# An LSTM layer on one core: twelve plain steps for sixteen, and one sigmoid for three gates of half the features

## The reference

```python
# x (32, 512, 512), h0 = cond_1024 (32, 512), Wx and Wh (512, 2048), b (2048,)
xW = jnp.einsum('ntd,dk->tnk', x, Wx) + b
def step(carry, xw_t):
    prev_h, prev_c = carry
    a = xw_t + prev_h @ Wh
    i = sigmoid(a[:, :H]); f = sigmoid(a[:, H:2*H]); o = sigmoid(a[:, 2*H:3*H])
    g = tanh(a[:, 3*H:])
    next_c = f * prev_c + i * g
    next_h = o * tanh(next_c)
    return ((next_h, next_c), next_h)
_, hs = lax.scan(step, (h0, 0), xW)
out = x + transpose(hs, (1, 0, 2))
```

## Time and profile before

| | |
|---|---|
| median of 3 runs | 2535.98 us (2535.93 to 2538.73) |
| the profiled execution's own time | 2535.94 us |
| its span | 2534.1 us |
| TensorE busy | 2515.8 us, 99% of the span |
| VectorE busy | 1983.6 us, 78% |
| ScalarE busy | 1247.9 us, 49% |
| chain that ended last | TensorE 98%, VectorE 1% |

### The profile page before, as it was taken

The page is one execution under the profiler, slowest core; times in us unless marked ns, Lnnn a source line. Parts: engine busy times, 40 slices in busy tenths (PEclk is TensorE's granted clock), DMA queues, the critical chain, the costliest instruction groups (busy, mean ns, idle before and its releaser), DMA issues.

```text
span 2534.1 us, 155783 instructions
## 1 busy us (share of the span) xinstructions
PE 2515.8 (99%) x67134; PEld 1795.3 (71%) x67134; DVE 1983.6 (78%) x8602; ACT 1247.9 (49%) x5266; POOL 7.2 (0%) x12
## 2 busy tenths in 40 slices
PE   8999999999999999999999999999999999999998
PEld 3577777777777777777777777777777777777775
DVE  7877777777777777777777777777777777777776
ACT  6544444444444444444444444444444444444443
POOL 1000000000000000000000000000000000000000
PEclk9999999999999999999999999999999999999999
DMA  8101101101011011010110110101101001011000
GB/s 234 37 20 30 33 17 33 28 21 33 17 33 33 17 33 25 24 33 17 33 33 17 33 25 25 33 17 33 33 17 33 25 25 33 17 33 33 17 17 18
DMA packets 142169, 80.21 MB, mean 32 GB/s; under 512 B 8620, under 2 KB 139836, under 8 KB 141372
## 3 DMA queue, kind: packets, MB, share of 16 engines
q1 hardware_dynamic: 140548, 75.40, 11.3%
q0 software_dynamic: 1152, 4.19, 0.9%
q10 hardware_dynamic: 440, 0.20, 0.0%
HBM read 42.02 MB, written 33.55 MB: 30 GB/s over the span
## 4 chain that ended last, share of the span: by engine, by line
PE 98%; DVE 1%; DMA 0%; ACT 0%; issue 0%; SPq 0%; DVEq 0%
PE even L327 26%; PE odd L327 26%; PE odd L321 26%; PE even L321 13%; PE s1t_sum L321 6%; DMA w_raw<-in_L_cond_Wx_dram 0%; DVE hw_lo L796 0%; PE odd L340 0%; PE plain_odd L327 0%; PE even L340 0%; PE plain_even L327 0%; PE plain_odd L340 0%; PE plain_even L340 0%; DVE xw_lo L796 0%; DVE f_c L709 0%
## 5 line engine op out<-in xcount | busy, mean ns | idle before, releaser
L709 DVE TENSOR_TENSOR f_c<-i_f,c_state 128x64 f32<-128x64 f32 x1024 | 233.0, 228 | 449.1 <-ACT i_f L561 449.1
L561 ACT ACTIVATE i_f<-odd 128x128 f32<-128x128 f32 x504 | 145.3, 294 | 536.8 <-PE odd L327 536.8
L327 PE MATMUL even<-hw_hi,hT_hi 128*32 128x512 f16 x4032 | 392.1, 379 | 2.4 <-issue 1.9
L327 PE MATMUL odd<-hw_hi,hT_hi 128*32 128x512 f16 x4032 | 392.1, 379 | 1.5 <-DVE hT_hi L658 1.5
L327 PE MATMUL even<-hw_lo,hT_hi 128*32 128x512 f16 x4032 | 392.1, 379 | 0.0
L327 PE MATMUL odd<-hw_lo,hT_hi 128*32 128x512 f16 x4032 | 392.1, 379 | 0.0
L321 PE MATMUL odd<-xw_hi,xT_hi 128*32 128x256 f16 x7936 | 388.6, 273 | 0.0
L321 PE MATMUL odd<-xw_hi,xT_lo 128*32 128x256 f16 x7936 | 388.6, 273 | 0.0
L321 PE MATMUL odd<-xw_lo,xT_hi 128*32 128x256 f16 x7936 | 388.6, 273 | 0.0
L561 ACT ACTIVATE i_f<-even 128x128 f32<-128x128 f32 x504 | 145.3, 294 | 426.1 <-PE even L327 426.1
L571 ACT ACTIVATE tanh_c<-c_state 128x64 f32<-128x64 f32 x1024 | 279.4, 273 | 99.8 <-DVE c_state L719 41.1
(11 more groups left out here) (127 smaller groups left out, 4098.0 us busy)
## 6 DMA issues: line engine op xcount, KB each, us to landing
x_ring<-in_x_dram SPq DMA_DIRECT2D x252, 128.0 KB, 2.8
out_dram<-x_ring SPq DMA_DIRECT2D x252, 128.0 KB
w_raw<-w_raw POOLq DMA_DIRECT2D x8, 512.0 KB, 5.9
w_raw<-in_L_cond_Wx_dram SPq DMA_DIRECT2D x3, 1024.0 KB, 9.4
w_raw<-in_L_cond_Wh_dram SPq DMA_DIRECT2D x3, 1024.0 KB, 15.5
w_raw<-in_L_cond_Wx_dram SPq DMA_DIRECT2D x2, 512.0 KB, 4.5
w_raw<-in_L_cond_Wh_dram SPq DMA_DIRECT2D x2, 512.0 KB, 19.4
x_ring<-in_x_dram SPq DMA_DIRECT2D x6, 64.0 KB, 18.1
```

The source lines that it names most:

```text
L327: mm = nc.tensor.matmul(bank[j * N:(j + 1) * N, :], hT[:, k * N:(k + 1) * N], w[:, k, j, :], start=False, stop=False, skip_group_check=True)
L561: nc.scalar.activation(i_f_half, bank_half, ACT.Sigmoid, scale=UNSCALE).then_inc(if_ready[two], 1)
L709: nc.vector.tensor_tensor(half_of(f_c[:, :], two), half_of(i_f[:, P:2 * P], two), half_of(c_state[:, :], two), ALU.mult)
```

## The change

- `PLAIN` is 12: steps 0 to 11 are plain, and pairs begin with step 12 (pair 6). The passes behind a `recur` are 11 a step until all 96 are done, in step 9.
- `REST_AT` is one step earlier for each piece: steps 4 to 11. `CAST_AT` and `NEGATE_AT` stay.
- ScalarE's and VectorE's written-out steps stay 16 (`UNROLLED`), TensorE's become 12.
- ScalarE takes i, f and o of one half of the features in one sigmoid of 128x192, in place of i and f of a half in one of 128x128 and o of all in one of 128x128 at the end. A step has four such instructions for gates in place of five. `tanh_c` is no longer behind o; `o_ready` goes.
- h0 is cast to `h_hi`, and its last quarter scaled to `h0_last`, by ScalarE in place of VectorE, ahead of ScalarE's `hw_hi`.
- `cast_plain(t)` of an even t waits for one transposed block of x in place of two. TensorE waits for `xp_hi` ahead of a step's passes, and for `xp_lo` only ahead of the last four of the twelve.
- `keep_going` comes once behind `spread_bias(0, 1)`, once ahead of the wait for h0's `hT_lo`, and twice behind each of k = 0 and 1; the one behind k = 2 goes.

```diff
-PLAIN = 16
+PLAIN = 12
...
-REST_AT = ((5, 5), (6, 6), (7, 7), (8, 8), (9, 9), (10, 10), (11, 11), (12, 12))
+REST_AT = ((4, 4), (5, 5), (6, 6), (7, 7), (8, 8), (9, 9), (10, 10), (11, 11))
...
+UNROLLED = -(-PLAIN // CHUNK) * CHUNK
...
-    return min(34 * step // 3, PASSES * (PLAIN - AHEAD)) if step < 13 else PASSES * (PLAIN - AHEAD)
+    return min(11 * step, PASSES * (PLAIN - AHEAD)) if step < PLAIN - 3 else PASSES * (PLAIN - AHEAD)
...
-        i_f = sb("i_f", [P, 2 * P], F32)
+        i_f_o = sb("i_f_o", [P, 3 * P], F32)
+        o_gate = i_f_o[:, 2 * P:3 * P]
...
                     if n % PASSES == 0 or n == first:
                         pe.wait_ge(plain_seeded, t + 1 - AHEAD)
+                        pe.wait_ge(xp_hi_ready, t + 1)
+                    if part == 2 and (k == 0 or n == first):
                         pe.wait_ge(xp_ready, t + 1)
...
                 plain_lo(1)
+                keep_going()
                 pe.wait_ge(hT_lo_ready, 1)
...
                     recur_add(bank, hT_hi, hw_lo, k)
-                    keep_going()
+                    if k < J - 2:
+                        keep_going()
+                        keep_going()
...
             spread_bias(0, 1).then_inc(bias_spread, 1)
+            keep_going()
...
             def cast_plain(t):
-                act.wait_ge(x_blocks_ready, blocks_count(t // GROUP, 2))
+                act.wait_ge(x_blocks_ready, blocks_count(t // GROUP, 1 + t % 2))
...
                 for two in range(2):
-                    i_f_half, bank_half = [a.rearrange("p (g e k) -> p g e k", g=2, k=J)[:, :, :, 2 * two:2 * two + 2]
-                                           for a in (i_f[:, :], bank[:, IF])]
-                    nc.scalar.activation(i_f_half, bank_half, ACT.Sigmoid, scale=UNSCALE).then_inc(if_ready[two], 1)
+                    i_f_o_half, bank_half = [a.rearrange("p (g e k) -> p g e k", g=3, k=J)[:, :, :, 2 * two:2 * two + 2]
+                                               for a in (i_f_o[:, :], bank[:, 0:3 * P])]
+                    nc.scalar.activation(i_f_o_half, bank_half, ACT.Sigmoid, scale=UNSCALE).then_inc(if_ready[two], 1)
                     nc.scalar.activation(half_of(g_gate[:, :], two), half_of(bank[:, 3 * P:4 * P], two), ACT.Tanh,
                                          scale=UNSCALE).then_inc(g_ready[two], 1)
-                nc.scalar.activation(o_gate[:, :], bank[:, 2 * P:3 * P], ACT.Sigmoid,
-                                     scale=UNSCALE).then_inc(o_ready, 1)
...
+            act.wait_ge(h0_loaded, 16)
+            nc.scalar.activation(h_hi[:, :], h0_raw[:, :], ACT.Copy).then_inc(h_hi_ready[0], 1)
+
+            nc.scalar.activation(h0_last[:, :], h0_raw[:, :].rearrange("p (e k) -> p e k", k=J)[:, :, J - 1], ACT.Copy,
+                                 scale=WSCALE).then_inc(h0_last_ready, 1)
...
-            dve.wait_ge(h0_loaded, 16)
-            nc.vector.tensor_copy(h_hi[:, :], h0_raw[:, :]).then_inc(h_hi_ready[0], 1)
```

More of the change, by code:

```diff
@@ L51 @@
 CAST_AT = (3, 4, 5, 6, 7, 8, 9, 10)
-REST_AT = ((5, 5), (6, 6), (7, 7), (8, 8), (9, 9), (10, 10), (11, 11), (12, 12))
+REST_AT = ((4, 4), (5, 5), (6, 6), (7, 7), (8, 8), (9, 9), (10, 10), (11, 11))
 BIAS_AT = 0
+UNROLLED = -(-PLAIN // CHUNK) * CHUNK
 AHEAD = 4
 PASSES = 12
-def passes_done(step):
-    return min(34 * step // 3, PASSES * (PLAIN - AHEAD)) if step < 13 else PASSES * (PLAIN - AHEAD)
 HALVED = (0, 7)
@@ L67, with passes_done @@
 F_EARLY, F_LATE = slice(0, 3), slice(4, 8)
+def passes_done(step):
+    return min(11 * step, PASSES * (PLAIN - AHEAD)) if step < PLAIN - 3 else PASSES * (PLAIN - AHEAD)
 def lstm_residual(nc, x, h0, w_x, w_h, bias, out):
@@ L125, in lstm_residual @@
         hT_lo = sb("hT_lo", [P, P], F16)
-        i_f = sb("i_f", [P, 2 * P], F32)
+        i_f_o = sb("i_f_o", [P, 3 * P], F32)
+        o_gate = i_f_o[:, 2 * P:3 * P]
         g_gate = sb("g_gate", [P, P], F32)
         s1t1 = sb("s1t1", [P, HALF], F32)
-        o_gate = sb("o_gate", [P, P], F32)
         c_state = sb("c_state", [P, P], F32)
@@ L198, in lstm_residual @@
         hT_hi_ready = [sem(f"hT_hi_ready{two}") for two in range(2)]
-        o_ready = sem("o_ready")
         h_full_ready = sem("h_full_ready")
@@ L573, in step @@
                 if plain_steps > AHEAD:
-                    act.wait_ge(o_ready, t + 1)
+                    act.wait_ge(g_ready[1], t + 1)
                     seed_plain(t + AHEAD)
@@ L646, in _ @@
                         cast_plain(t)
+            act.wait_ge(h0_loaded, 16)
+            nc.scalar.activation(h_hi[:, :], h0_raw[:, :], ACT.Copy).then_inc(h_hi_ready[0], 1)
+            nc.scalar.activation(h0_last[:, :], h0_raw[:, :].rearrange("p (e k) -> p e k", k=J)[:, :, J - 1], ACT.Copy,
+                                 scale=WSCALE).then_inc(h0_last_ready, 1)
             for k in range(J):
                 split_h_hi(k)
-            for t in range(PLAIN):
+            for t in range(UNROLLED):
                 step(t, t % CHUNK, CHUNK, t // CHUNK)
-            steps(mybir.EngineType.Activation, step, begin=PLAIN // CHUNK)
+            steps(mybir.EngineType.Activation, step, begin=UNROLLED // CHUNK)
         @block.vector
@@ L708, in forget @@
                 dve.wait_ge(if_ready[two], count)
-                nc.vector.tensor_tensor(half_of(f_c[:, :], two), half_of(i_f[:, P:2 * P], two),
+                nc.vector.tensor_tensor(half_of(f_c[:, :], two), half_of(i_f_o[:, P:2 * P], two),
                                         half_of(c_state[:, :], two), ALU.mult)
@@ L713, in remember @@
                 dve.wait_ge(g_ready[two], count)
-                nc.vector.tensor_tensor(half_of(i_g[:, :], two), half_of(i_f[:, 0:P], two), half_of(g_gate[:, :], two),
+                nc.vector.tensor_tensor(half_of(i_g[:, :], two), half_of(i_f_o[:, 0:P], two), half_of(g_gate[:, :], two),
                                         ALU.mult).then_inc(i_g_ready[two], 1)
@@ L840, in _ @@
             transpose_h(h_lo_ready, h_lo, hT_lo, hT_lo_ready, 1)
-            nc.vector.tensor_scalar(out=h0_last[:, :], in0=h0_raw[:, :].rearrange("p (e k) -> p e k", k=J)[:, :, J - 1],
-                                    scalar1=WSCALE, scalar2=None, op0=ALU.mult).then_inc(h0_last_ready, 1)
             dve.wait_ge(h0_last_ready, 1)
@@ L848, in _ @@
             dve.wait_ge(c_zeroed, 1)
-            for t in range(PLAIN):
+            for t in range(UNROLLED):
                 step(t, t % CHUNK, CHUNK, t // CHUNK)
-            steps(mybir.EngineType.DVE, step, begin=PLAIN // CHUNK)
+            steps(mybir.EngineType.DVE, step, begin=UNROLLED // CHUNK)
 _INS = ['x', 'cond_1024', 'L0_cond_Wx', 'L0_cond_Wh', 'L0_cond_b']
```

## The result

| | before | after |
|---|---|---|
| median, 18 runs of each | 2536.52 us (2535.84 to 2538.73) | 2541.32 us (2539.50 to 2543.31) |
| ratio | | 1.0016, 95% interval 1.0010 to 1.0023 |
| the profiled execution's own time | 2535.94 us | 2543.31 us |
| its span | 2534.1 us | 2539.9 us |

The changed kernel is 4.8 us slower by the medians, 0.19% of them; the ratio on record is 1.0016. That is within what the prediction called no measurable change, though the interval doesn't reach 1 and so the slowdown is clear of the noise of 18 runs. It is inside the predicted range (2536.3 to 2542.5); of the forecast and the rivals it lies nearest to the one in which the clock falls (2540.6). The sum of 2538.7 us was 2.6 short.

The account below looks back on a forecast made before the run. TensorE's own list of groups, without idle time in the loop, was taken as the bound. Terms -1.2 + 0.3 - 0.44 - 0.12 + 0.4 + 3.75 = +2.7 us on 2535.94 gave 2538.7 us, range 2536.3 to 2542.5.

Parts of the forecast that it names:

- the likeliest case: Whole kernel: the forecast by the sum of terms, 2538.7 us, within 2537.3 to 2539.8; chance 0.63.
- the clock's rival: TensorE's wait ahead of step 12: clock falls to half, +1.3 to +2.6 us, 2540.6 us; chance 0.16.
- two pairs for four plain steps: Steps 12 to 15 on TensorE: become two pairs, each 0.6 us shorter than two plain steps, -1.2 us.
- waits for the state at the end: Last two recurrent parts and last gates: TensorE waits 0.105 us longer three times, +0.3 us.
- head and step 1: Start of kernel: VectorE's `hw_lo` ends 0.44 us sooner, step 1's recurrent part comes 0.12 us nearer.
- wait for S2's lo part, step 10: Ahead of step 10's `middle`: VectorE makes the lo part late, so TensorE waits, +0.4 us.
- wait for A22, to VectorE's end and handover: Ahead of step 12's recurrent part: TensorE stands still for A22's last lo part, +3.75 us.
- A + 5.77: VectorE finishes A22's last lo part 5.77 us after A, the start of step 11's first sigmoid.
- With the handover `recur(12)` begins at A + 5.82: Step 12's recurrent part on TensorE starts 5.82 us after step 11's first sigmoid begins, in place of 2.07.
- One sigmoid for three gates: Gates of each step: the state's chain gets 0.105 us longer, costing nothing in the loop.
- the slack of 0.17: Loop: first half of `hT_hi` is ready 0.17 us a step before TensorE needs it, handover allowed for.
- The rival of the chain: Loop: delay exceeds the slack, TensorE waits in 250 odd steps, 7.5 us at the upper bound, 2546.2 us; chance 0.13.

Follow-up runs that it names:

- experiment 6: Changed kernel with 16 plain steps and the old `passes_done` and `REST_AT`, so only head and gates differ from the kernel before: 2534.17 us, ratio 0.9989.
- the last kernel of experiment 7: Changed kernel with the waits for A22's and S2's lo parts moved to their uses and TensorE's steps 12 to 15 written out: 2533.21 us, ratio 0.9986.
- experiment 1: Changed kernel with TensorE's wait for A22's lo part moved from ahead of step 12 into `close_odd`, where A22 is used: 2534.13 us, ratio 0.9989.
- experiment 2: Changed kernel with 15 groups of matmuls on zeros ahead of the wait for A22's lo part: 2537.71 us, ratio 1.0004.
- experiment 3: Changed kernel with TensorE's steps 12 to 15 written out behind the unmoved wait for A22, loop beginning with step 16: 2538.57 us, ratio 1.0007.
- experiment 4: Changed kernel with sixty small matmuls on zeros at the start of TensorE's program, wait for A22 not filled: 2539.61 us, ratio 1.0011.
- Experiment 5: Its first kernel: experiment 1 plus one extra 128x64 tanh on ScalarE between the two halves of each step: 2554.24 us, ratio 1.0071.
- experiment 5's last kernel: The kernel before with the one sigmoid for three gates and nothing else changed: 2536.76 us, ratio 1.0000.

## Why the prediction was right, and where it was not

It was right in the sign, in the place and in the cause of the largest term; of the likeliest case one term was too small, the clock was given to a rival, and a gain of 2.1 us was not seen. That the time lies near the clock's rival is partly luck: the two terms that no case had, +1.4 and -2.1, nearly cancel. Term by term, from the trace of the changed kernel and, where marked, of an experiment:

| term | predicted | measured |
|---|---|---|
| two pairs for four plain steps | -1.2 | -1.1 |
| waits for the state at the end | +0.3 | +0.5 |
| head and step 1 | -0.56 | -0.58 (experiment 6) |
| wait for S2's lo part, step 10 | +0.4 | +0.49 |
| wait for A22, to VectorE's end and handover | +3.75 | +3.7 |
| late start behind it | none | +1.4 |
| clock at 1.2 GHz behind it | rival, +1.3 to +2.6 | +2.4 |
| stop behind the end of the loop | none | -2.1 |
| **sum** | **+2.7** | **+4.7** |

The wait for S2's lo part is there as forecast, though the page calls it "issue":

```profile
81.08 0.40 PE L322 MATMUL s1t_sum<-xw_hi,xT_hi 128*32 128x256 f16 x8 [0.77 <-issue]
```

The first measured term is what is left of the table of steps: from step 2 to the end the difference grows by 5.76 - 0.49 = 5.27 us, and the other terms without the head make 0.5 + 0.49 + 3.7 + 1.4 + 2.4 - 2.1 = 6.4, so -1.1 remains. As a remainder it is no test of the forecast; the last kernel of experiment 7 is one. It gains 0.70 us from step 2 to step 507, after losses of 0.17 from step 10 to 11 (4.86 us, against 4.69 from step 14 to 15 before) and 0.32 at the entry, so the two pairs give 1.2 there. The sum agrees with the medians' +4.8. In the prediction, 2535.94 and its terms make 2538.6 and not 2538.7.

**The wait for A22.** The method held: VectorE's own list gave A + 5.77 for the end, the trace has 91.27 - 85.54 = A + 5.73. Its size as idle time was off, 4.95 us in place of 3.75, because the term ended at the handover. The step of the prediction that failed is "With the handover `recur(12)` begins at A + 5.82": it assumed that TensorE's next instruction is at hand. It began at A + 7.19. Experiments 1 to 4 show the parts, and that moving the wait takes all of it away.

**The clock.** The rival with 0.16 is what happened, at the upper part of its range. I had argued from one fall, 4.8 us behind the last matmul, that 3.75 us were safe. One case bounds nothing: it was 3.0 us here (87.78 to 90.8). The +2.4 is of one execution, the longest of 18. The Trainium skill (TensorE: Matmul & The Clock Gate, "Why this matters for your kernels") warns of idle gaps between bursts of matmuls; with the groups of 0.43 us behind the gap this trace agrees, and the rule should have had more weight than one row.

**One sigmoid for three gates.** Right. In the loop of the changed kernel ScalarE and VectorE show:

```profile
1011.02 0.35 ACT L568 ACTIVATE i_f_o<-odd 128x192 f32<-128x192 f32 x1 [2.17 <-PE odd L328]
...
1011.36 0.37 ACT L568 ACTIVATE i_f_o<-odd 128x192 f32<-128x192 f32 x1
```

```profile
1011.75 0.24 DVE L719 TENSOR_TENSOR f_c<-i_f_o,c_state 128x64 f32<-128x64 f32 x1
...
1012.71 0.24 DVE L668 STREAM_TRANSPOSE hT_hi<-h_hi 128x64 f16<-128x64 f16 x1
```

The sigmoids stand 0.34 apart (predicted 0.335), `f_c` of the second half begins at A + 0.73 (0.715), the transpose ends at A + 1.93 (1.95). TensorE takes it at A + 2.07, less the handover 2.01: 0.07 to 0.08 of the slack of 0.17 is left. Experiment 5 tests that: 0.10 us more on the chain (0.43 between the sigmoids, not 0.34) makes a step 0.038 longer, so some 0.06 were free. The rival of the chain was rightly held unlikely, and the row of 192 elements was the right one to go by. Its price was counted wrongly, for odd steps alone: where the chain did become the bound, even and odd steps lost alike, so 0.03 us beyond the slack would be some 15 us and not 7.5 (an estimate from that experiment). At the end the 0.1 shows at each wait for the state (+0.29, +0.10 and +0.11 by the steps' table), together 0.2 more than three times 0.105; what makes the first of these 0.29 is open.

**The head.** The gain is there but not in the profile of the changed kernel:

```profile
16.57 2.00 ACT L615 ACTIVATE xw_hi<-w_raw 128x1024 f16<-128x1024 f32 x2 [1.53 <-DMA w_raw<-in_L_cond_Wx_dram]
```

```profile
20.91 9.68 DVE L806 SCALAR_TENSOR_TENSOR hw_lo<-w_raw,hw_hi 128x512 f16<-128x512 f32 x16
```

```profile
19.82 9.69 DVE L806 SCALAR_TENSOR_TENSOR hw_lo<-w_raw,hw_hi 128x512 f16<-128x512 f32 x16
```

The first two are of the changed kernel, the third of experiment 6. The last weights for x landed at 16.55, in the profile of before at 15.39. `hw_lo` ends at 30.59 and not near 29.5, 1.1 late for a load that was 1.16 late. In experiment 6, with the same head and a landing at 15.45, `hw_lo` begins at 19.82 where it was 20.25: 0.43 sooner, predicted 0.44. Over the twelve profiles the landing lies between 15.4 and 16.9, among kernels with the same head too, so a single profile can't be read to 1 us there.

**The end of the loop.** The 2.1 us at step 508 are a stop of 1.92 us behind the loop's exit which the kernel before has and no kernel with the new head or fewer plain steps has; only experiment 5's last kernel, the one that is the old one in all but the gates, has it. It was in the trace of before, in the chain of waits as idle time with nothing waited for, and I passed it by since no edit was near. That the stops depend on where code lies in TensorE's program is shown by experiment 4 for the one at the loop's entry (1.4 and 0.29 us beyond the handover, for one and the same work; experiment 3 has no entry at that place). Kernels with the same TensorE program agree, at the entry (0.56, 0.55, 0.55 us) and at the exit (1.92, 1.98). For the stop at the exit it is argued from where it appears, and the number of instructions ahead can't be all of it: experiments 2 and 4 both have sixty matmuls more than the changed kernel, yet step 509 comes 5.61 us after step 508 in experiment 2, with an idle time of 0.47 us in `s1t_sum`, and 5.14 in experiment 4, where the loop has 4.88.

That instructions are fetched late is a likely thought, but it isn't shown. The traces list the DMAs that load instructions, and at the entry they speak against it. In the changed kernel they have not one packet from 84.5 to 93.6 us, so no load was under way in the late start from 91.3 to 92.7. At the exit they leave it possible: one packet of instructions begins between 2510.0 and 2511.1 in the kernel before, which stops from 2510.56 to 2512.48, and one between 2510.5 and 2511.5 in experiment 5's last kernel, which stops from 2511.04 to 2513.02. But one begins between 2517 and 2518 in the changed kernel too, and nothing stops. What makes TensorE stand still, and which position costs how much, stays open.

## What to carry to other kernels

Put a wait directly ahead of the first instruction that uses the data, not at a seam of the program: here the seam stood a recurrent part and more ahead of the use, and cost 7.2 us, more than all the rest of the change could give. Price an idle time of TensorE by what follows it too, the late start and the groups at 1.2 GHz, and don't take one observed fall of the clock as a bound on when it falls. When a change alters the length of an engine's program, look in the trace for idle time with nothing waited for: it may go or come anywhere, and 2 us of it can hide or feign a result.

## What the runs showed of the hardware that I had not expected

- TensorE starts up to 1.4 us late at the entry of a loop, and stood still for 1.9 to 2.0 us just behind the exit of one, with no semaphore that the profile shows and no load of instructions under way in the former. Sixty small matmuls far ahead took the first from 1.4 to 0.3 us beyond the handover. Time spent waiting before doesn't cover it: with a wait of 3.7 us it was 1.4, without one (experiment 1) 0.75.
- The clock fell 3.0 us after the last matmul in one kernel, 4.5 and 4.2 in two others (experiments 3 and 4), there only after the matmuls had begun again, 2.2 in experiment 5's last kernel, and 4.8 at the end of the kernel before. An idle time of 3.6 to 3.8 us brought 3.4 us at 1.2 GHz, one of 4.95 brought 6.8. An idle time of 1.92 us behind the loop brought none in the kernel before, and one of 1.98 at the same place in experiment 5's last kernel brought 3.4 us. Each of these is one execution; the spread of the spans (3.0 us over ten executions in experiment 3, 0.9 over eleven in experiment 1) suggests that it differs from one execution to the next.
- A chain that is 0.04 us too long in every step shows in no idle column; it seems to make some matmuls longer (382 ns for 379), and only the distance of steps far apart (0.038 us a step, 18.84 us over the loop) gives it away.
